# Reading the last chunk's pair products back from DRAM with two issuing engines: SyncE and ScalarE in place of SyncE alone

## The reference

```
e = [tbl_f[ids[:, f]] for f in 26 features]             # (512, 26, 64)
x = layer_norm(dense @ Wd.T)                            # (512, 128)
y = layer_norm(e @ Ws.T); y = einsum("bne,pn->bep", y, Wsi)
y = swapaxes(layer_norm(y), 1, 2)                       # (512, 32, 128)
T = concat([x, y])                                      # (512, 33, 128)
Z = T @ T.T                                             # (512, 33, 33), the pair products
o = layer_norm(tril(Z) @ Wl.T)[:, :384]                 # 528 pairs to 512 columns
h = relu(concat([o, dense]) @ W_top1 + b_top1)
h = relu(h @ W_top2 + b_top2)
out = h @ W_top3                                        # (512, 1)
```

## Time and profile before

| | |
|---|---|
| Median of three timed runs | 259.2 us (258.77, 259.23, 259.20) |
| Span of the profiled execution | 258.3 us |
| PE busy | 183.6 us (71%) |
| PEld busy | 117.3 us (45%) |
| DVE busy | 100.9 us (39%) |
| ACT busy | 90.1 us (35%) |
| POOL busy | 101.3 us (39%) |
| PE's share of the chain that ended last | 52% |
| DMA read from and written to HBM | 9.29 MB and 2.16 MB |

### The profile page before, as it was taken

One profiled execution on the slowest core, in us unless ns is written; L12 is line 12 of the kernel. 1 busy time (PEld: TensorE's weight loads), 2 busy tenths in 40 slices (PEclk: granted clock), 3 DMA queues, 4 the chain that ended last, 5 costly groups with the idle time before them and its releaser, 6 DMA issues.

```text
span 258.3 us, 4239 instructions
## 1 busy us (share of the span) xinstructions
PE 183.6 (71%) x1616; PEld 117.3 (45%) x1616; DVE 100.9 (39%) x193; ACT 90.1 (35%) x221; POOL 101.3 (39%) x113
## 2 busy tenths in 40 slices
PE   1696913859295662948487569574849989999996
PEld 1343903516144252625264433443446466649476
DVE  2766003361078270526263401615254288623120
ACT  2442100710073340636034302523235276522333
POOL 4887772777405265445373720727250000000000
PEclk9999555695779595698777959859597999999999
DMA  6423235111100011015210100134110004123000
GB/s 171 150 67 111 56 107 173 28 27 25 20 1 19 15 21 22 10 20 129 41 23 10 33 10 0 22 94 68 21 25 0 0 0 116 27 86 53 3 0 0
DMA packets 19391, 11.67 MB, mean 45 GB/s; under 512 B 14256, under 2 KB 16816, under 8 KB 19376
## 3 DMA queue, kind: packets, MB, share of 16 engines
q1 hardware_dynamic: 16048, 8.05, 11.5%
q0 software_dynamic: 3328, 3.41, 6.9%
HBM read 9.29 MB, written 2.16 MB: 44 GB/s over the span
## 4 chain that ended last, share of the span: by engine, by line
PE 52%; issue 21%; another core or an unknown queue 13%; DVE 8%; ACT 4%; DMA 1%; SPq 0%; ACTq 0%; DVEq 0%
PE proj_ps L482 12%; PE dots_ps L473 8%; PE o_ps L501 6%; PE mix_ps L450 4%; PE quad_ps L461 4%; DVE var_p L786 2%; PE proj_ps L518 2%; PE turn_ps L501 2%; PE turn_ps L442 1%; PE proj_ps L396 1%; PE o_ps L505 1%; PE mix_ps L518 1%; PE o_ps L551 1%; PE dots_ps L551 1%
## 5 line engine op out<-in xcount | busy, mean ns | idle before, releaser
L373 POOL DMA_INDIRECT e_rows<-table_dram,rows_sb x104 | 100.5, 966 | 90.3 <-DVE e_unit L822 59.6
L473 PE MATMUL dots_ps<-feats 128*32 128x33 f32 x1024 | 27.0, 208 | 46.1 <-issue 45.9
L482 PE MATMUL proj_ps<-f_sb,proj_w 128*128 128x512 f32 x64 | 47.2, 878 | 5.7 <-issue 3.2
L473 PEld LDWEIGHTS dots_ps<-feats 128*32 128x32 f32 x1024 | 18.5, 117 | 55.8 <-issue 54.0
L786 DVE TENSOR_REDUCE var_p<-y_sq 128x16 f32<-128x512 f32 x32 | 21.4, 683 | 24.3 <-ACT y_sq L616 21.5
L818 DVE RECIPROCAL rstd_n<-std_n 128x8 f32<-128x8 f32 x16 | 3.2, 201 | 66.3 <-ACT std_n L636 61.5
L450 PE MATMUL mix_ps<-mixw_sb,e_unit 128*128 128x192 f32 (+4 forms) x128 | 21.7, 315 | 10.3 <-DVE e_unit L822 10.3
L616 ACT ACTIVATE y_sq<-proj_ps 128x512 f32<-128x512 f32 x32 | 18.7, 595 | 28.0 <-PE proj_ps L482 14.5
L482 PEld LDWEIGHTS proj_ps<-f_sb,proj_w 128*128 128x128 f32 x64 | 15.4, 266 | 22.8 <-issue 17.1
L450 PEld LDWEIGHTS mix_ps<-mixw_sb,e_unit 128*128 128x128 f32 x128 | 20.4, 201 | 11.0 <-DVE e_unit L822 10.9
L461 PEld LDWEIGHTS quad_ps<-gram,e_cols 128*128 128x128 f32 x104 | 18.5, 244 | 12.2 <-issue 12.1
(11 more groups left out here) (131 smaller groups left out, 179.2 us busy)
## 6 DMA issues: line engine op xcount, KB each, us to landing
z_dram<-z_mine SPq DMA_DIRECT2D x4, 512.0 KB
e_rows<-table_dram,rows_sb POOLq DMA_INDIRECT x104
w_sb<-w_dram SPq DMA_DIRECT2D x2, 512.0 KB, 4.7
wl_sb<-wl_dram SPq DMA_DIRECT2D x2, 512.0 KB
w_sb<-w_dram SPq DMA_DIRECT2D x1, 768.0 KB
z_pairs<-z_dram SPq DMA_DIRECT2D x12, 64.0 KB
dense_sb<-dense_t_dram SPq DMA_DIRECT2D x1, 512.0 KB
wl_sb<-wl_dram SPq DMA_DIRECT2D x1, 256.0 KB
```

The costliest lines, as they stand in the source:

```text
L373: pool.indirect_dma_start(out=e_rows[:, t, D * ab:D * (ab + 1)], out_offset=None, in_=table, in_offset=bass.IndirectOffsetOnAxis(ap=rows_s ...
L473: mm = pe.matmul(dots_ps[PR * k:PR * (k + 1), (PR + 1) * g:(PR + 1) * (g + 1)], f[:, 2:PR + 2], f[:, 0:PR + 1], start=True, stop=True)
L482: pe.matmul(proj_ps[:, ab, :], proj_w[:], f_sb[:, q % 2, ab, :], start=True, stop=True).then_inc(projected, 1)
```

## The change

The seven reads of the last chunk are dealt out. SP issues the pieces 0, 2 and 4. ACT issues the read of the sums and the pieces 1, 3 and 5. ACT's four stand at the head of its tail, ahead of `square_o` of chunk 2, behind a wait for the two writes of the last chunk. The reads of the other three chunks stay with SP. What is read, and where to, is the same.

```diff
+        def read_piece(eng, chunk, pairs_on_rows, piece, semaphore):
+            t, row, band, pair, number = piece
+            eng.dma_start(pairs_on_rows[row:row + number, t, :, :],
+                          z_dram[bass.ds(chunk, 1), band, :, :].rearrange(
+                              "s (k p) (c g) -> (s p c) k g", k=4, g=PR)[pair:pair + number, :, :]
+                          ).then_inc(semaphore, 16)
+
+        def read_moments(eng, chunk, semaphore):
+            eng.dma_start(moments[0:PR, bass.ds(chunk, 1), :, :].rearrange("p s k g -> p (s k) g"),
+                          s_dram[bass.ds(chunk, 1), :, :].rearrange("s (k p) g -> p (s k) g", k=4)
+                          ).then_inc(semaphore, 16)
...
             write_z(CHUNKS - 1)
-            read_z(CHUNKS - 1, z_last, z_last_moved)
+            for piece in PIECES[0::2]:
+                read_piece(sp, CHUNKS - 1, z_last, piece, z_last_moved)
             sp.wait_ge(y_done, 1)
...
+            act.wait_ge(z_out, CHUNKS * 32)
+            read_moments(act, CHUNKS - 1, z_last_moved)
+            for piece in PIECES[1::2]:
+                read_piece(act, CHUNKS - 1, z_last, piece, z_last_moved)
             square_o(CHUNKS - 2)
             root_o(CHUNKS - 2)
             scale_o(CHUNKS - 2)
```

More of the change, by code:

```diff
@@ L333, in read_z @@
             def read_z(chunk, pairs_on_rows, semaphore):
[L334 to L341, removed]
+                for piece in PIECES:
+                    read_piece(sp, chunk, pairs_on_rows, piece, semaphore)
+                read_moments(sp, chunk, semaphore)
             write_z(0)
```

## The result

The changed kernel took 263.28 us (median of 4 runs, 261.84 to 264.60) against 258.99 us before (4 runs, 258.02 to 259.23): a ratio of 1.0169, 95% interval 1.0118 to 1.0219. It is slower by 4.3 us; 264.0 was forecast.

What follows compares the result with a forecast made beforehand. The prediction took PE's own chain to bound the tail, fed by ACT's `o_sq`. Delay 3.1 us plus half-rate clock 1.7 us made 4.8, on a median of 259.2: 264.0 us, range 261.6 to 266.5.

Steps and rivals of the forecast that it cites:

- What bounds the tail: From about 194 us on, PE's own work at full clock bounds the end; any wait of PE is paid in full.
- The 0.16 us of slack at turn_o(2): Chunk 2's chain from `o_sq` to PE's turn_o(2) could slip 0.16 us before it delays PE.
- The gain at zero: Last chunk's reads land about 1 us sooner, worth 0, since top_1 covers them and PE does not wait.
- The wait, 1.0 us: ACT's wait for `z_out` ahead of chunk 2's `o_sq` takes 1.01 us from it.
- The four issues, 2.25 us: ACT's four DMA issues ahead of `o_sq` at SP's pace, 0.51 + 3 x 0.58 us; `o_sq` starts 3.26 us later.
- held-up rival: SP's and ACT's issues go one after the other, ACT free at 237.06 at the latest: 265.8 us, chance 0.19.
- the 3.1 forecast: turn_o(2) and all PE work behind it move by 3.1 us, after ACT's wait and issues less the slack.
- The clock, 1.7 us: PE's idle gap brings one 3.4 us stretch at half clock from about when PE resumes, costing 1.7 us.
- The rival with twice that length: Half rate lasts two stretches, 6.8 us, if the clock falls within PE's wait; costs 2.9 us: 265.2 us, chance 0.13.
- Clock kept: Rival: the clock does not fall in the tail, so only the 3.1 us delay is paid: 262.3 us, chance 0.15.
- Faster: Rival: PE waits for the reads at linear(3)'s head in timed runs; earlier landing brings up to 1 us: 258.2, chance 0.02.
- no change: Rival: `z_out` full and ACT's four issues through before 232.2, so PE is not delayed; chance 0.02.

Runs made afterwards that it cites:

- the trial of the wait alone: Changed kernel with SP issuing all seven reads again and ACT keeping only its wait for `z_out`; ratio to the kernel before 1.0024 (medians 259.41 and 258.94).
- without the wait: Changed kernel with ACT's four transfers reading chunk 2's earlier-written data, so the wait for the last chunk's write falls away; ratio to the kernel before 0.9988.
- the three matmuls: Changed kernel with three matmuls, results thrown away, added on PE ahead of turn_o(2); ratio to the kernel before 1.0198, beside 1.0229 for the changed kernel.
- the trial with seven issues: Changed kernel with all seven reads issued by ACT behind the same wait, none by SP; ratio to the kernel before 1.0258 (medians 266.05 and 259.35).
- the third profile: Changed kernel itself, unaltered, profiled and timed once more on another chip; ratio to the kernel before 1.0229.
- the one with four on POOL: Changed kernel with ACT's four transfers issued by POOL instead, on a semaphore of their own, ACT as before; ratio to the kernel before 1.0102.

## Why the prediction was right, by its own steps

**What bounds the tail.** Right that PE's own chain does, and that `o_sq` feeds it. The 0.16 us of slack at turn_o(2) was misread: they are the end of one matmul running over the start of the next, and PE's weight load was itself already waiting 0.16 us for `o_unit`. Each delay of `o_sq` reached linear(3) whole, to 0.02 us: 0.97 gave 0.96 in the trial of the wait alone, 0.37 gave 0.35 without the wait, 3.58 gave 3.56 with the three matmuls. Nor is it right that the clock was at full from 194 us on: it was at half until 197.0, and one of the last ten slices reads 7. The tail from there is 61 us at full, as the argument needs.

**The gain at zero.** Right. The reads were in some 2.4 us sooner in the trial without the wait, and linear(3) did not start sooner.

**The wait, 1.0 us.** Right: 0.97 in the trial, 232.27 - 228.16 - 3.07 = 1.04 in the changed kernel. The write took 3.71 us from its issue to the first read, 3.68 before.

**The four issues, 2.25 us.** Slightly too low: 2.56 (234.83 - 232.27). I had taken SP's mean. The first two took 0.41 and 0.50, the last two 0.70 and 0.80. Of the 0.31 us too little, 0.24 went with SP reading at the same time (2.07 against 1.83 us for the same three pieces); it is far from the held-up rival, whose upper end was 4.0. With no slack to take off, PE's delay was 3.6 us, for the 3.1 forecast: 0.31 from the issues, 0.16 from the slack, the rest from rounding and the wait.

**The clock, 1.7 us.** Right in two profiles of three, where one stretch of 3.4 us at half began about as PE resumed. The rival with twice that length happened in the third, and in the trial with seven issues, and its price was right too: in the third profile the tail grew by 6.7 us for 3.8 of delay, which leaves 2.9. The granted clocks of the timed runs agree: (1 - clock) x 2 x span is the time at half, 87 us in the mean of the 23 runs of the kernel before beside the first trials, 90.7 and 89.5 in the first 4 and the 6 later runs of the changed one. That is 2 to 4 us more at half, so 1 to 2 us of loss. Single runs scatter by some 3 us around these means, so that this does not tell in how many executions the stretch falls.

**The sum.** The tail grew by 5.3 us where 4.8 were forecast. The timed medians grew by 4.3 and 3.6 us on the chips of 259 us, and by 3.9 on the third (in the runs that its ratio uses). Of the difference 0.3 us is found: the timed value stands 2.1 us above the span in the kernel before, and 1.8 in the kernels with DMAs on ACT (and in the one with four on POOL). Against the first two medians 0.7 and 1.4 us are not found; 5.3 - 0.3 = 5.0 lies inside the first interval of the ratio and at the edge of the second. Executions in which the clock keeps full would give such a remainder, and three profiles cannot exclude that there are some. So that 264.0 came within 0.8 us of 263.28 is in part luck: the delay was put 0.5 us too low, and the timed runs lost less than the profiled tail. The base was also off: going by those 2.1 us, the profiled execution of before, with its span of 258.3, took some 260.4 us itself (an estimate), and I had set its span 0.9 us under the median as if it were an average one. That does not touch the forecast, which was made as a difference on the median.

**The rivals.** Held-up issues, one after the other: excluded, since SP's three and ACT's four were through in 2.56 us together and seven on ACT alone took 4.10; the small slowing that is left is 0.24 us. Clock kept: seen in no profile of the changed kernel, not excluded for other executions. Faster, no change: nothing speaks for them.

## What to carry to other kernels

Ask of each transfer that is to land sooner who stands still for it now; here the one engine that idled on it was not on the path. A DMA issue is an instruction in its engine's program, here with about 0.6 us of that engine's time and with its wait: behind a wait it blocks all that follows, and the same four issues with their wait made ACT's next step 3.6 us late ahead of a chain that PE needs, and cost 0.6 us behind it, which the timed runs could not tell from nothing. When a wait of some microseconds is opened in a stretch where PE has run without a gap, look at the granted clock of the next rows as well: here that added 1.7 us to a wait of 3.4, and 2.9 in one profile.

## What the runs showed of the hardware that I had not expected

The kernel before took 258.9 and 259.4 us on two chips and 194.3 on a third, where the changed one took 198.2 (the last two as above). The page's group of the small matmuls of `dots` shows one difference (busy, mean ns, then idle time before them and what ended it), first for the changed kernel on a chip of 259 us, then on that of 194:

```profile
L481 PE MATMUL dots_ps<-feats 128*32 128x33 f32 x1024 | 26.5, 206 | 43.8 <-issue 43.7
```

```profile
L481 PE MATMUL dots_ps<-feats 128*32 128x33 f32 x1024 | 13.8, 207 | 0.0
```

In every profile of the first two chips PE idled 43 to 47 us ahead of these matmuls, nearly all of it for nothing that the profile shows; on the third it idled 1.3 us at most. What it waits for there is open. The other difference is the clock: by the sum above the kernel before was at half rate for 87 us on the first two chips and for 26 on the third. The tail, which is a straight piece of program, was the same on all of them to 0.2 us, and so was the delay that the change brings.

The clock fell within PE's wait in two profiles (the third of the changed kernel, the seven on ACT) and about its end in the first two of the changed kernel. Where it fell 0.9 or 1.6 us before PE resumed, the half rate held for 6.8 us; where it fell 0.2 us before that or 0.6 behind, for 3.4. Four profiles do not make a rule of it.
